# A transformer stack on one core: the causal mask of self attention, by TensorE or by VectorE

## What is computed

```
b, s, d = x.shape                                   # 2, 1024, 256; 16 heads of 16
qkv = jnp.einsum('bsd,hde->bhse', x, Wqkv) + bqkv[None, :, None, :]
q, k, v = jnp.split(qkv, 3, axis=-1)
score = jnp.einsum('bhsd,bhtd->bhst', q, k)
causal = jnp.tril(jnp.ones((s, s), dtype=bool))
score = jnp.where(causal[None, None], score, -jnp.inf)
attn = jax.nn.softmax(score / jnp.sqrt(jnp.asarray(HEAD_DIM, x.dtype)), axis=-1)
y = jnp.einsum('bhst,bhtd->bhsd', attn, v)
```

## Time and profile before

| | us |
|---|---|
| median of 3 runs | 1470.11 |
| lowest, highest | 1466.77, 1473.82 |
| the profiled execution | 1470.0 |
| its span, first to last instruction | 1468.2 |
| the stretch of the maxima | 70.94 to 302.90 |
| the tail of the self attention | to about 332 |

### The profile page before, as it was taken

How to read it: one execution, slowest core, us unless ns; L and a number is a source line. 1 busy time by engine, 2 the same in 40 slices (tenths; PEclk the granted TensorE clock), 3 DMA queues, 4 the chain that set the end, 5 groups by cost and what they waited for, 6 DMA issues and landing times. The chain is left out here.

```text
span 1468.2 us, 27608 instructions
## 1 busy us (share of the span) xinstructions
PE 1304.5 (89%) x9691; PEld 1035.2 (71%) x9691; DVE 1019.2 (69%) x2014; ACT 882.9 (60%) x2217; POOL 457.7 (31%) x626
## 2 busy tenths in 40 slices
PE   5989999999599999978899866589989599999997
PEld 3534444436489999866788644368877599999995
DVE  5687877825456566546866897678875688888773
ACT  5426667674466666535221266378873688888883
POOL 5312222229133333323100255511110334444320
PEclk9979999999999999998999987689998799999998
DMA  3756324100100000003000210021111677777755
GB/s 89 224 79 156 44 45 65 25 2 5 30 1 2 2 1 2 1 5 118 0 1 1 66 30 1 22 53 44 45 24 42 193 233 229 233 235 232 230 167 186
DMA packets 97916, 116.15 MB, mean 79 GB/s; under 512 B 23549, under 2 KB 83187, under 8 KB 97779
## 3 DMA queue, kind: packets, MB, share of 16 engines
q1 hardware_dynamic: 88323, 99.83, 25.7%
q0 software_dynamic: 4416, 12.06, 2.6%
q10 hardware_dynamic: 5040, 2.49, 0.6%
HBM read 88.47 MB, written 16.55 MB: 72 GB/s over the span
## 5 line engine op out<-in xcount | busy, mean ns | idle before, releaser
L827 ACT ACTIVATE sa_probs<-ps 128x512 f32<-128x512 f32 (+1 forms) x304 | 154.5, 578 | 87.8 <-PE ps L780 86.7
L851 DVE TENSOR_REDUCE sa_top<-ps 128x2 f32<-128x1024 f32 (+3 forms) x160 | 171.9, 1114 | 40.9 <-PE ps L756 26.3
L3133 ACT ACTIVATE room<-ps,cx_top 128x154 f32<-128x154 f32 x256 | 97.0, 388 | 89.8 <-DVE cx_top L3197 89.8
L2670 PE MATMUL ps<-me_h,me_w_parts 128*128 128x256 f32 x1104 | 140.3, 287 | 4.9 <-issue 3.0
L2670 PEld LDWEIGHTS ps<-me_h,me_w_parts 128*128 128x128 f32 x1104 | 136.8, 192 | 6.4 <-issue 3.2
L2684 PE MATMUL ps<-me_w_parts,me_mid 128*128 128x256 f32 x1104 | 136.5, 283 | 0.0
L2684 PEld LDWEIGHTS ps<-me_w_parts,me_mid 128*128 128x128 f32 x1104 | 132.6, 189 | 0.0
L2995 POOL TENSOR_TENSOR room<-room 128x512 f32<-128x512 f32 x64 | 66.7, 1042 | 169.8 <-DVE room L3205 169.7
L2751 DVE TENSOR_TENSOR me_w_parts<-me_chunk,me_w_parts 128x1024 fp32r<-128x1024 f32 x92 | 110.4, 1222 | 9.5 <-ACT me_w_parts L2711 7.4
L2735 ACT ACTIVATE me_full<-ps,me_b 128x256 f32<-128x256 f32 x184 | 94.6, 514 | 34.8 <-PE ps L2670 34.8
L2781 DVE TENSOR_TENSOR me_mid<-me_full,me_mid 128x256 fp32r<-128x256 f32 x184 | 90.2, 508 | 34.8 <-ACT me_mid L2737 31.5
(11 more groups left out here) (460 smaller groups left out, 3425.1 us busy)
## 6 DMA issues: line engine op xcount, KB each, us to landing
me_chunk<-in_L_ffn_W_dram SPq DMA_DIRECT2D x92, 512.0 KB
sa_k<-scr_k SPq DMA_DIRECT2D x48, 128.0 KB, 4.6
sa_q<-scr_q SPq DMA_DIRECT2D x96, 64.0 KB, 4.7
cn_qd<-cn_qh SPq DMA_DIRECT2D x60, 64.0 KB, 2.1
scr_q<-room SPq DMA_DIRECT2D x6, 512.0 KB, 4.9
scr_k<-room SPq DMA_DIRECT2D x6, 512.0 KB, 5.3
me_b<-in_L_ffn_b_dram SPq DMA_DIRECT2D x23, 128.0 KB, 3.6
x<-in_x_dram SPq DMA_DIRECT2D x4, 512.0 KB, 6.2
```

Source lines behind the costliest of these rows:

```text
L827: act.activation(probs[:, step % self.PROBS, h0:h0 + many, 0:w], src[:, :, 0:w], ACT.Exp, scale=DH ** -0.5).then_inc(exped.sem, 1)
L851: dve.tensor_reduce(top2[:, k % 2, k0 // 512, h0:h0 + many, sb % HBLK], src[:, :, 0:w], AX.X, ALU.max).then_inc(freed.sem, 1)
L2670: last = pe.matmul(ps[:, MID + n % 4, 0:RT], w[:, u % 2, 0, i, DM * k + P * b:DM * k + P * b + P], h[:, u % 2, j, k, :], start=(m == 0), s ...
L3133: last = act.activation(p[:, h + i, :], ps[:, S_BANK + n % SR, M * i:M * i + M], ACT.Exp, bias=top[:, t % 2, h + i:h + i + 1], accum_out=d ...
```

## The change

TensorE no longer adds the mask: each head's product ends its accumulation at once. VectorE, once the piece is `filled`, adds `maxmask` (repeated over the heads) in place in PSUM to the last 128 columns of each head, waits until that is done (`masked`), and then takes the maximum. The planner's costs are as they were.

```
             rows_in = [c.sig(f"sa_rows_in{i}") for i in range(self.NEGS)]
+            masked, self.diagonals = c.sig("sa_masked"), 0
...
                         out = take(use["piece", k, n])
-                        diagonal = k0 + w == (sb + 1) * P
                         q0 = P * (sb - HBLK * half)
                         for j in range(many):
                             a = 1024 // many * j
                             last = pe.matmul(out[:, a:a + w], self.q_st[0:96, slot, half, h0 + j, q0:q0 + P],
-                                             self.k_st[0:96, slot, h0 + j, k0:k0 + w], start=True, stop=not diagonal)
-                            if diagonal:
-                                last = pe.matmul(out[:, a + w - P:a + w], c.identb[:, :], c.maxmask[:, :], start=False,
-                                                 stop=True)
+                                             self.k_st[0:96, slot, h0 + j, k0:k0 + w], start=True, stop=True)
                         last.then_inc(filled.sem, 1)
...
                         src = area(m).rearrange("p (j s) -> p j s", j=many)
+                        if k0 + w == (sb + 1) * P:
+                            block = src[:, :, w - P:w]
+                            dve.tensor_tensor(block, block, c.maxmask[:, :].unsqueeze(1).to_broadcast([P, many, P]), ALU.add
+                                              ).then_inc(masked.sem, 1)
+                            self.diagonals += 1
+                            dve.wait_ge(masked.sem, masked.at(self.diagonals))
                         dve.tensor_reduce(top2[:, k % 2, k0 // 512, h0:h0 + many, sb % HBLK], src[:, :, 0:w], AX.X, ALU.max
                                           ).then_inc(freed.sem, 1)
```

More of the change, by code:

```diff
@@ L888, in run @@
             for x, n in ([(filled, total), (freed, total), (s_chain, self.chained), (s_parts, NSUB), (scored, chunk0[-1]),
-                          (exped, chunk0[-1]), (weighed, step0[-1]), (copied, NSUB), (inverted, NSUB), (joined, len(UNITS)), (selected, HBLK * NSUB)]
+                          (exped, chunk0[-1]), (weighed, step0[-1]), (copied, NSUB), (inverted, NSUB), (masked, self.diagonals), (joined, len(UNITS)), (selected, HBLK * NSUB)]
                          + [(x, 16 * PARTS * len(range(i, NSUB, self.NEGS))) for i, x in enumerate(rows_in)]):
```

## The result

The changed kernel takes 1495.17 us (median of 4 runs, 1494.69 to 1495.74) where the kernel before takes 1470.04 (4 runs). The ratio is 1.0169, 95% interval 1.0150 to 1.0187: 25 us slower. The forecast was 1489 with a range of 1477 to 1504, and 90% on slower. The direction, the main mechanism and the range held; the forecast was 6 us low, and two of its errors cancel in part, as the account behind the experiments shows.

The account below looks back on a forecast made before the run. TensorE was taken to set the pace in the self attention's maxima, VectorE not far behind. The larger engine time per 4 us window summed to 250.9 us, 19.0 more, so 1470.0 + 19.0 = 1489 us, range 1477 to 1504.

Parts of the forecast that it names:

- The price of an addition: Each of 96 VectorE additions before diagonal maxima: 0.424 us (256 elements) or 0.691 (512), plus 0.03 of wait.
- The sum: Self attention's stretch of maxima: the larger of TensorE's and VectorE's time per window, 250.9 us in all, 19.0 more.
- VectorE's demand: VectorE's work in the stretch of maxima: 184.8 us plus 52.1 for the additions, 236.9 us.
- The change of the bound: In the stretch of maxima TensorE falls from 232.0 to 217.2 us, VectorE rises to 236.9 and becomes the bound.
- The unevenness: VectorE must idle at times in the stretch of maxima, as order and two areas are fixed: 14.1 us.
- windows of 4 us: Chosen width over which two waiting areas and one in work average the stretch of maxima; gives +19.0 us.
- Deeper averaging: Rival, 12%: in the maxima pieces come early enough that VectorE nearly always finds one; 1475 to 1480 us.
- stay the bound: Rival, 3%: the additions fit into VectorE's idle time among the maxima and TensorE's 14.8 us gain is kept; 1462 us.
- The clock: Rival, 13%: an idler TensorE falls to 1.2 GHz more often in the maxima, 14 us on top of 19; 1503 us.
- my signs of being wrong: Additions below 0.35 us, VectorE's gaps as long while TensorE waits too, or the stage's clock row falling from 0.96.
- four new falls: Further drops of TensorE's clock among the maxima, 3 to 4 us lost at each, 14 us together.
- A low stretch: One spell of TensorE at 1.2 GHz among the maxima: some 8 us, giving 4 us' worth of its work.

Follow-up runs that it names:

- e1: The changed kernel without VectorE's additions, so neither engine adds the mask in the first pass; 1462.0 us, ratio 0.9949 to the kernel before.
- e2: The changed kernel with TensorE's 256 mask products kept beside VectorE's additions; 1500.2 us, ratio 1.0207 to the kernel before.
- e9: The changed kernel with a second addition, over the last 64 columns and with its own wait, behind each first; 1531.3 us, ratio 1.0421 to the kernel before.
- e3_half_mask: The changed kernel with each addition over the last 64 columns of the diagonal block instead of 128; 1483.0 us, ratio 1.0088 to the kernel before.
- e6: The changed kernel with TensorE's mask products kept in the first three half units alone (56 of 256); 1498.5 us, ratio 1.0188 to the kernel before.
- e4: The changed kernel with its instruction list planned for VectorE's additions, plus a rule against circular waits; 1517.5 us, ratio 1.0333 to the kernel before.

## Why the prediction was right, and what was off

**The price of an addition** held: 425 and 693 ns against 424 and 691, taken from rows that read PSUM and write SBUF. That the output lies in PSUM costs nothing.

**The sum, term by term.** The stretch was to last 250.9 us: 236.9 of VectorE's work, its waits included, and 14.0 in which it idles. It lasted 255.3: 233.9 of work (230.6 busy and 96 waits of 0.034 us) and 21.4 idle. So the work was put 3.0 us too high and the idle time 7.4 us too low. That the two cancel in part is luck; the remaining 1.5 us of the miss lie in the layers behind.

**VectorE's demand** came out 3.4 us lower, or 3.0 with the wait at 0.034 us. Its busy time rose by 230.6 - 184.8 = 45.9 us, and 96 waits of 0.03 us make it 48.8, not 52.1. The reason is in the earlier trace rows too. The durations of the additions add up to 49.4 us and those of the maxima are what they were (178.3 and 178.6 us). What grew is the overlap of neighbouring instructions, from 8.1 to 12.0 us: an instruction that follows one on VectorE without a pause starts some 0.08 us early. That this comes from VectorE having been idle before many diagonal pieces, and no longer being so, is the likely reading and was not counted.

**The change of the bound** held: removing TensorE's 14.8 us of products is worth 11.4 us of stretch when VectorE has nothing added (e1) and 2.6 when it has (e2). It did not go wholly: behind the start a third of the relief still counts, as e2 shows.

**The unevenness** was the mis-sized term: 14.0 us of idle time for VectorE, where 21.4 were measured. I took windows of 4 us as what two areas can average over and said that this was a choice. The sum itself was also made otherwise than its text says, in two ways that pull against each other. As TensorE's time it took not the window's length but TensorE's busy time in it; done so, the unchanged kernel would have a stretch of 228.3 us, where it has 232.0. And it took each window's count of mask products as printed, where a product that reaches over an edge stands in both windows: 270 products in windows of 4 us and 280 in windows of 2.5, instead of 256. The table has the sums as they were made (for e9, and the narrow ones for e1 and e2, behind their runs), and the sums made as the text says, with each product counted once, behind all runs:

| change of the stretch, us | 4 us, as made | 2.5 us, as made | 4 us, counted once | 2.5 us, counted once | measured |
|---|---|---|---|---|---|
| changed | +19.0 | +24.1 | +16.8 | +21.9 | +23.4 |
| e2_both | +20.6 | +26.0 | +19.8 | +24.1 | +26.0 |
| e3_half_mask | +2.5 | +7.2 | +2.5 | +6.9 | +7.8 |
| e9_more | +54.6 | +60.6 | +49.8 | +55.2 | +59.3 |
| e1_no_mask | -18.1 | -17.4 | -14.9 | -13.8 | -11.4 |

The 2.5 us as made come within a microsecond and a half wherever there are additions, but in part by the double counting. Counted once, they fall short by 1 to 4 us, and with VectorE's demand as measured they give +18.8 for the changed kernel, 4.6 short. The narrow windows are nearer than those of 4 us in every row, so two engines with two areas average over less than I took. The width of 2.5 us was picked from the outcome, and which width is right is not shown. Nor is my reading that it stands for two areas without the one in work (a piece and its share of the rest takes 1.45 us).

Without additions (e1) the sum for 2.5 us as made misses by 6 us, counted once by 2.4. For what is left I can argue a reason but did not test it: where TensorE gets faster, it meets an area that is not yet free. Its waits for areas rose from 32.6 to 42.1 us in e1.

**The rivals.** Deeper averaging did not happen. TensorE did not stay the bound. The clock: one of my signs of being wrong did come, as its row in the stretch fell from 0.96 to 0.93. Among the maxima it falls to 1.2 GHz twice as before, earlier and for longer, and nowhere else, so that the low time is 34 us instead of 21; from 120 us on it is at 2.4 GHz to the end of the self attention, even behind a window of 4 us with TensorE busy 2.79:

```profile
128.00:132.00 4.00, 2.79 (x18) 1.22 (x15) 3.90 (x6) 2.80 (x7) 1.28 (x2) 1.00 0.43 89
```

So the price of four new falls was not paid. What the longer low stretches cost can be bounded, not told: 15.8 of the 23.4 us come without any, and between e2 and e6 the same instructions differ by 3.7 us. Two sizes in that rival were off. A low stretch was put at 8 us from windows that cut it at both ends; the clock's records give 10.2 us to each of the two before, and 20.5 and 13.7 us now. And 8 us at 3.7 in 4.3 hold 6.9 us of full-clock work, not 7.4.

## What to carry to other kernels

Before work is moved to an engine that idles a quarter of the time, look at where it idles: cut the stage into short windows, add the larger of the two in each, and take several widths as a range, since the right one isn't known ahead (here 4 us fell short and 2.5 us came nearer). Count each instruction once, and check that the same sum gives the present time when nothing is changed. Work can be cheap where it stands because it is pipelined (0.058 us of TensorE for a 128-column product) and dear elsewhere (0.18 to 0.23 us of VectorE for the same columns). And ask whether the work is needed at all: the maximum that steadies a softmax is free to be taken over more keys than the softmax has.

## What was not expected of the hardware

The same instructions ran with the clock back at 2.4 GHz at 111.9 us in one profiled execution (e2) and at 118.2 in another (e6). The low stretch had begun within 0.5 us of the same time in both (105.0 and 104.5), so its end differs by 6 us between executions whose instructions up to there are the same. In the changed kernel the clock stayed at 2.4 GHz behind 4 us with TensorE busy 2.79 (128 to 132), and in e4 it fell behind 4 us with 2.56 busy (244 to 248, already at 0.95 there).

VectorE's addition in place in PSUM takes 425 and 693 ns for 256 and 512 elements, the time of one that writes to SBUF (424 and 691). Waiting for it costs 0.034 us, and the instruction behind it loses the 0.08 to 0.09 us by which it would have started early.
